# A two-layer kernel with routed experts: layer 1 rows go to a fixed region per expert, in three routing batches

## The reference

```python
router_logits = h @ Wr + br                       # [2048, 8]
gates = max(softmax(router_logits)); idx = argmax(router_logits)
xn = layernorm(h) * ln_g + ln_b
y = (relu(xn @ W1[idx] + b1[idx]) @ W2[idx] + b2[idx]) * gates
x = x + gb * y
```

## Time and profile before

| | before |
|---|---|
| median of 3 runs | 422.17 us |
| the profiled execution | 422.7 us, of which 420.7 us lie between the first and the last instruction (the span) |
| PE busy, PEld busy | 309.1 us (73%), 226.5 us (54%) |
| DVE busy | 288.0 us (68%) |
| ACT busy | 173.2 us (41%) |
| POOL busy | 189.0 us (45%) |
| mean granted TensorE clock | 0.774 |

### The profile page before, as it was taken

The page is one execution under the profiler, slowest core; times in us unless marked ns, Lnnn a source line. Parts: engine busy times, 40 slices in busy tenths (PEclk is TensorE's granted clock), DMA queues, the critical chain, the costliest instruction groups (busy, mean ns, idle before and its releaser), DMA issues.

```text
span 420.7 us, 7639 instructions
## 1 busy us (share of the span) xinstructions
PE 309.1 (73%) x2168; PEld 226.5 (54%) x2169; DVE 288.0 (68%) x819; ACT 173.2 (41%) x333; POOL 189.0 (45%) x318
## 2 busy tenths in 40 slices
PE   1784889888991789969779799988877000999960
PEld 1582316734240333258679799976565000989960
DVE  7587993889379999438885567635895860578850
ACT  1124563223750217885255355546255210545520
POOL 8573782390037670000267545455143474045450
PEclk9877555555595555888999999999996555799995
DMA  2499900000001112001121422158800123233310
GB/s 83 66 353 368 322 22 1 0 2 1 2 21 44 44 51 35 0 2 42 49 65 55 80 72 63 37 166 240 248 2 1 43 85 101 61 87 87 86 47 0
DMA packets 37805, 32.93 MB, mean 78 GB/s; under 512 B 10765, under 2 KB 28770, under 8 KB 37776
## 3 DMA queue, kind: packets, MB, share of 16 engines
q1 hardware_dynamic: 33792, 25.10, 21.6%
q0 software_dynamic: 3936, 7.49, 5.6%
q10 hardware_dynamic: 48, 0.00, 0.0%
HBM read 19.50 MB, written 13.98 MB: 80 GB/s over the span
## 4 chain that ended last, share of the span: by engine, by line
PE 45%; DVE 27%; issue 8%; DMA 5%; POOL 5%; ACT 4%; SPq 2%; DVEq 2%; POOLq 0%
PE ps L1353 9%; PE ps L1364 8%; PE ps L1181 6%; PE ps L1176 5%; DVE mx L1958 5%; PE ps L1156 4%; POOL rows L624 4%; PE ps L1203 2%; PE ps L1132 2%; ACT wide L855 2%; DVE hb L2094 2%; SPq L302 2%; DVE ps L2220 1%; PE ps L1337 1%; DMA rows<-token_rows,posu 1%
## 5 line engine op out<-in xcount | busy, mean ns | idle before, releaser
L624 POOL DMA_INDIRECT rows<-token_rows,posu x48 | 50.2, 1046 | 52.5 <-DVE posu L1855 25.5
L636 POOL DMA_INDIRECT back<-ys,places x39 | 38.6, 990 | 75.0 <-DVE ys L2105 69.8
L1364 PE MATMUL ps<-w_out,hg 128*128 x496 | 65.2, 276 | 0.0
L1364 PEld LDWEIGHTS ps<-w_out,hg 128*128 128x128 f32 x496 | 60.1, 192 | 0.2
L2094 DVE TENSOR_TENSOR hb<-ps,b_in 128x512 f32<-128x512 f32 x62 | 42.6, 687 | 25.4 <-PE ps L1353 25.2
L953 ACT ACTIVATE hg<-hb 128x512 f32<-128x512 f32 x62 | 39.1, 630 | 38.8 <-DVE hb L2094 35.0
L1958 DVE TENSOR_REDUCE mx<-ps 128x2 f32<-128x512 f32 (+2 forms) x48 | 44.4, 949 | 5.4 <-PE ps L1156 5.1
L1353 PE MATMUL ps<-xsT,w_now 128*128 128x128 f32 x256 | 38.3, 297 | 6.5 <-DVE hb L2094 4.1
L1337 PE MATMUL ps<-ident,xs 128*128 128x128 f32 x62 | 17.7, 292 | 33.9 <-DMA xs<-rows 33.9
L1156 PE MATMUL ps<-feat,qs 64*128 64x281 bf16 (+2 forms) x128 | 33.3, 431 | 12.0 <-DVE mx L1958 7.6
L839 ACT COPY qs<-ps 128x768 bf16<-128x768 bf16 (+1 forms) x21 | 15.3, 728 | 59.6 <-PE ps L1132 59.6
(11 more groups left out here) (404 smaller groups left out, 588.0 us busy)
## 6 DMA issues: line engine op xcount, KB each, us to landing
rows<-blank SPq DMA_DIRECT2D x20, 260.0 KB, 7.1
xs<-rows SPq DMA_DIRECT2D x62, 64.0 KB, 1.9
w_in<-in_L_ffn_w_fc SPq DMA_DIRECT2D x1, 2048.0 KB, 14.9
w_in<-in_L_ffn_W SPq DMA_DIRECT2D x1, 2048.0 KB, 10.6
rest<-rows SPq DMA_DIRECT2D x23, 65.0 KB, 1.9
token_rows<-in_L_attn_x SPq DMA_DIRECT2D x1, 832.0 KB, 8.3
wmod<-in_L_wmod SPq DMA_DIRECT2D x2, 384.0 KB, 4.5
rows<-token_rows,posu POOLq DMA_INDIRECT x48, 2.4
```

The lines of the kernel that those rows point to most:

```text
L624: pool.indirect_dma_start(ROWS[l], bass.IndirectOffsetOnAxis(ap=posu[:, k, j:j + 1], axis=0), token_rows[:, j, 0:WIDTH[l]], None).then_inc ...
L636: pool.indirect_dma_start(where, bass.IndirectOffsetOnAxis(ap=target[r] if l else places[:, t, :].bitcast(U32)[:, 0:1], axis=0), ys[:, r, ...
L1364: mm = pe.matmul(ps[:, 6 + c % 2, 0:D], hg[:, c % RING, n * P:(n + 1) * P], w_out[:, bass.ds(e * NB + n, 1), :], start=(n == 0), stop=(n = ...
```

## The change

1. `rows1` gets a region of 2048 rows for each of the 8 experts and one spare block: 129 blocks of 128 rows in place of 23. A row's place is 2048 times its expert plus its rank, so no total is needed before rows are sent. All 129 blocks are cleared; the clearing of `rows1` moves behind the loads of layer 0's expert weights on SP.
2. Layer 1 is routed in three batches (token tiles 0-2, 3-10, 11-15). PE sums a row's rank in PSUM (`regions`, `rank`); DVE has `choose_one`, `place_one`, `gate_one` for each batch. The scale arithmetic is shared out anew between POOL and DVE, and the rows of the last two pieces that DVE normalised are ACT's now.
3. `plan_tiles` on DVE writes, for each of the 23 tiles, the number of its block to `src_tile`. SP reads this number into a register (`value_load`) for each tile; its loop over layer 1 tiles is written out as `second_tiles`, with `xs` and `rest` of **the same tile** in one step.
4. The gate row that multiplies `w_out` in `gate_weights(1)` is read from PSUM.
5. Some semaphores are merged, and `rows_dve` replaces two.

```diff
+BATCHES = [(0, 3), (3, 11), (11, 16)]
+BATCH_OF = [0, 1, 1, 2, 2]
+SPARE = NE * NT
...
-            return -(-NTILE[l] * WIDTH[l] // (4 * ROW0))
+            return -(-(SPARE + 1 if l else T0) * WIDTH[l] // (4 * ROW0))
...
             clear_rows(sp, 0)
+            load_experts(sp, 0)
             clear_rows(sp, 1)
-            load_experts(sp, 0)
...
-                def next_rest(k, c):
-                    if l:
-                        sp.wait_ge(sem(f"ys_sent{c % RING}"), 16 * (k + (c // RING + 1 + earlier(l, c % RING))))
-                        load_rest(k + 1, c)
...
+            def second_tiles():
+                src = ROWS[1].rearrange("(t p) c -> p t c", p=P)
+                at = [None] * T1
+                def load_rest(t):
+                    sp.dma_start(rest[t % RING][:], src[:, bass.ds(at[t], 1), D:D + REST]).then_inc(
+                        sem(f"rest_loaded{t % RING}"), 16)
+                sp.wait_ge(sem("placed"), 4)
+                for t in range(RING):
+                    at[t] = sp.value_load(src_tile[0:1, t:t + 1], min_val=0, max_val=SPARE)
+                sp.wait_ge(sem("scattered_all"), 16 * NT)
+                for t in range(RING):
+                    load_tile(1, at[t], t)
+                for t in range(RING):
+                    load_rest(t)
+                for t in range(RING, T1):
+                    at[t] = sp.value_load(src_tile[0:1, t:t + 1], min_val=0, max_val=SPARE)
+                    sp.wait_ge(sem("xs_used"), T0 + t - RING + 1)
+                    load_tile(1, at[t], t)
+                    sp.wait_ge(sem(f"ys_sent{t % RING}"), 16 * (t // RING + earlier(1, t % RING)))
+                    load_rest(t)
+            first_tiles()
+            second_tiles()
...
-            def step_scales(c, summed, done):
-                lo, hi = STEPS[c]
-                scales(SLOT_OF[lo], SLOT_OF[lo] + hi - lo, summed, done, c + 1)
-            for c in range(3):
-                step_scales(c, "summed_1", "scaled_1")
-            pool.wait_ge(sem("summed_1"), 5)
-            root(8, 13).then_inc(sem("roots"), 1)
-            for c in range(2):
-                step_scales(c, "summed_2", "scaled_2")
-            pool.wait_ge(sem("slots_all"), 1)
-            pool.wait_ge(sem("gates_all"), 1)
+            scales(*STEPS[0], "summed_1", "scaled_1", 1)
+            scales(*STEPS[1], "summed_1", "scaled_1", 2)
+            scales(*STEPS[0], "summed_2", "scaled_2", 1)
+            scales(*STEPS[2], "summed_1", "scaled_1", 3)
+            scales(*BATCHES[2], "summed_1", "scaled_1", 4)
+            scales(*STEPS[1], "summed_2", "scaled_2", 2)
             pool.wait_ge(sem("cleared1"), 16 * clears(1))
             for c, (lo, hi) in enumerate(STEPS):
...
+                pool.wait_ge(sem("placed"), BATCH_OF[c] + 1)
+                pool.wait_ge(sem("gates_all"), BATCH_OF[c] + 1)
...
             step_rows(0)
             keep_x(0)
             step_rows(1)
             keep_x(1)
             modulated(1)
+            step_sent(0)
             step_rows(2)
+            keep_x(2)
+            gate_exp(0)
             modulated(2)
-            keep_x(2)
+            step_rows(3)
+            step_rows(4)
             modulated(3)
             modulated(4)
-            act.wait_ge(sem("rows1_dve"), 3)
             keep_x(3)
             keep_x(4)
-            step_sent(0)
-            act.wait_ge(sem("lg_shifted"), 1)
-            act.activation(lg2[:], lg2[:], ACT.Exp).then_inc(sem("lg_exp"), 1)
-            for c in range(1, len(STEPS)):
-                step_sent(c)
+            gate_exp(1)
+            step_sent(1)
+            step_sent(2)
+            gate_exp(2)
+            step_sent(3)
+            step_sent(4)
+            act.copy(ps[:, 6, 0:D], modrow[1][:, GB, :]).then_inc(sem("row_placed"), 1)
...
+            def regions(b):
+                lo, hi = BATCHES[b]
+                pe.matmul(ranks(b), onesb[:], region[:].unsqueeze(1).to_broadcast([P, hi - lo, NE]), start=True, stop=False)
+                for j in range(lo):
+                    pe.matmul(ranks(b), onesb[:], picked(j, hi - lo), start=False, stop=False)
+            def rank(b):
+                lo, hi = BATCHES[b]
+                pe.wait_ge(sem("chosen"), 3 + b)
+                for j in range(lo, hi - 1):
+                    pe.matmul(ranks(b)[:, j + 1 - lo:hi - lo, :], onesb[:], picked(j, hi - 1 - j), start=False, stop=False)
+                pe.matmul(ranks(b), before[:], chosen[:, lo:hi, :], start=False, stop=True).then_inc(sem("ranked"), 1)
...
             modes_out(4)
+            pe.wait_ge(sem("x_kept"), 6)
+            logits(0, 0)
             turn_back(1)
-            pe.wait_ge(sem("x_kept"), 6)
-            logits(0)
-            logits(1)
+            pe.wait_ge(sem("chosen"), 3)
+            regions(0)
+            rank(0)
             turn_f(2)
-            logits(2)
+            pe.wait_ge(sem("placed"), 1)
+            logits(1, 1)
+            logits(1, 2)
+            turn_back(2)
+            pe.wait_ge(sem("x_kept"), 7)
+            regions(1)
             turn_f(3)
             turn_f(4)
-            logits(3)
-            logits(4).then_inc(sem("logits1"), 1)
-            for c in (2, 3, 4):
-                turn_back(c)
-            count("all")
+            rank(1)
+            logits(2, 3)
+            logits(2, 4)
+            pe.wait_ge(sem("rows_all"), 1)
+            regions(2)
+            turn_back(3)
+            turn_back(4)
+            pe.wait_ge(sem("rows_all"), 2)
+            totals(0, BATCHES[2][0])
+            rank(2)
+            totals(BATCHES[2][0], NT).then_inc(sem("ranked"), 1)
...
-                gb = modrow[l][:, GB, :].unsqueeze(1)
+                gb = ps[:, 6, 0:D].unsqueeze(1) if l else modrow[l][:, GB, :].unsqueeze(1)
+                if l:
+                    v.wait_ge(sem("row_placed"), 2)
...
+            def choose_one(b):
+                lo, hi = BATCHES[b]
+                n = hi - lo
+                bc = lambda t: t.unsqueeze(2).to_broadcast([P, n, NE])
+                c, l, m = cand[:, lo:hi, :], lg2[:, lo:hi, :], top[:, 0, lo:hi]
+                pl = ps[:, 0, 0:n * NE].rearrange("p (j e) -> p j e", e=NE)
+                v.wait_ge(sem("logits1"), b + 1)
+                then(v.tensor_reduce(m, pl, AX.X, ALU.max))
+                signal(v.tensor_tensor(l, pl, bc(m), ALU.subtract), "lg_shifted", b + 1)
+                then(v.scalar_tensor_tensor(out=c, in0=l, scalar=0.0, in1=e_rank[:].unsqueeze(1).to_broadcast([P, n, NE]), op0=ALU.is_equal, op1=ALU.mult))
+                then(v.tensor_reduce(posf[:, lo:hi], c, AX.X, ALU.max))
+                signal(v.tensor_tensor(chosen[:, lo:hi, :], c, bc(posf[:, lo:hi]), ALU.is_equal), "chosen", 3 + b)
+            def place_one(b):
+                lo, hi = BATCHES[b]
+                v.wait_ge(sem("ranked"), b + 1)
+                then(v.tensor_tensor(cand[:, lo:hi, :], ranks(b), chosen[:, lo:hi, :], ALU.mult))
+                then(v.tensor_reduce(posf[:, lo:hi], cand[:, lo:hi, :], AX.X, ALU.add))
+                signal(v.tensor_copy(posu[:, 0, lo:hi], posf[:, lo:hi]), "placed", b + 1)
+            def gate_one(b):
+                lo, hi = BATCHES[b]
+                v.wait_ge(sem("lg_exp"), b + 1)
+                then(v.tensor_reduce(posf[:, lo:hi], lg[:, lo:hi, :], AX.X, ALU.add))
+                signal(v.reciprocal(token_rows[:, lo:hi, GATE], posf[:, lo:hi]), "gates_all", b + 1)
+            def plan_tiles():
+                bank, at = TOTALS_AT
+                v.wait_ge(sem("ranked"), 4)
+                c = cmp_f[:].rearrange("p (e j) -> p e j", e=NE)
+                then(v.tensor_tensor(c, ps[:, bank, at:at + NE].unsqueeze(2).to_broadcast([P, NE, NT]),
+                                     step128[:].unsqueeze(1).to_broadcast([P, NE, NT]), ALU.is_gt))
+                then(v.tensor_reduce(ntile[:], c, AX.X, ALU.add))
+                running(bound[:, 0:NE], ntile[:], 0.0)
+                then(v.tensor_scalar(slack[:], ntile[:], -1.0, float(NT), ALU.mult, ALU.add))
+                then(tile_experts(0, T1, NE))
+                c = cmp_e[:, 0:T1 * NE].rearrange("p (t n) -> p t n", n=NE)
+                then(v.tensor_tensor(c, c, slack[:].unsqueeze(1).to_broadcast([P, T1, NE]), ALU.mult))
+                then(v.tensor_reduce(srcf[:, 0:T1], c, AX.X, ALU.add))
+                then(v.tensor_tensor(srcf[:, 0:T1], srcf[:, 0:T1], tidx[:, 0:T1], ALU.add))
+                signal(v.tensor_scalar(src_tile[:, 0:T1], srcf[:, 0:T1], float(SPARE), None, ALU.min), "placed", 4)
...
+            sent_sums(0, ("summed_2", 1))
+            step_sums(2, 3)
             step_sums(3)
-            step_sums(4)
-            for c in range(2):
-                sent_sums(c, ("summed_2", c + 1))
-            v.wait_ge(sem("roots"), 2)
-            for c in (3, 4):
-                for j in range(*STEPS[c]):
-                    at = SLOT_OF[j]
```

(77 more changed lines are left out.)

223 lines of the change are left out of this document (102 added, 121 removed).

## The result

The changed kernel takes 550.51 us (median of 4 runs, 545.89 to 552.98), the kernel before 422.89 us beside it (4 runs): a ratio of 1.312, interval 1.302 to 1.322. The profiled execution took 549.4 us, with a span of 547.7.

A forecast was written before the change was run, and what follows sets the result against it. Bound by a chain through POOL's scatter queue, then the expert loop at 2.01 us a tile. Span 420.7 - 8.9 + 133.0 + 2.5 = 547.3, plus 1.5 to the runs' median: 549 us, range 526 to 568.

The forecast's parts named there:

- SP's order makes the loop a ring: Layer 1 expert loop: SP's wait for a tile's send stands ahead of the next tile's xs; +133.0 us.
- Rival 3: SP in layer 1's loop isn't held by send waits, only the routing saving is left; 413 us, chance 0.05.
- Length of the way: Layer 1 loop, transpose to next transpose through down, DVE, POOL's send, rest and xs: 9.45 us at low clock.
- The register load: SP, between rest and xs: reading the block number adds 0.35 us, DVE's price; that step becomes 1.0 us.
- Rival 2: SP's read of the block number costs PE's maximum, 1.26 us; 565 us, chance 0.07.
- The clock: PE in layer 1's loop: granted 0.50 through idling; down takes 1.92 instead of 1.06 us, the transpose 0.11 more.
- Rival 1: PE keeps a granted clock of 1.00 in layer 1's loop, 8.48 us a step; 530 us, chance 0.18.
- The routing's gain: Before layer 1's loop: POOL's last scatter starts at 343.3 instead of 352.16; 8.9 us saved, bounds 11.2 and 7.5.
- the wait for piece 2's second turn: Layer 1 routing, DVE waiting for PE: end at 321.4, bounds 319.1 and 322.75; fourth scatter starts at 327.9.
- The stretched scatters: POOL, layer 1: two scatters of 2.01 and 1.90 us instead of 0.96 end with PSUM operand; saving 5.5 if they stay.
- The clearing: Clearing 129 blocks of rows1: ends near 91 us under idle DMA, costs nothing; 38 us without that cover.
- The tail: End of layer 1's loop: five down and two up remain, the first three or so at low clock; +2.5 us.

The follow-up runs named there:

- the run with added work: Changed kernel with 36 identity transposes added on PE ahead of the first product of 16 layer 1 tiles; 538.9 us, ratio 1.277.
- lead of 4: Changed kernel with only SP's loop put back: behind xs of tile t the wait and rest of tile t - 4; 415.53 us, ratio 0.985.
- the gate row: Version with a lead of 4, the row multiplying w_out in layer 1 read from SBUF as in the kernel before; 417.76 us, ratio 0.992.
- the turn put first: Version with a lead of 4, PE's turn_back(2) moved ahead of logits(1, 2); 413.35 us, ratio 0.980.

## Why the prediction was right, step by step

Predicted 549 us, measured 550.5; the sum was made against the span, 547.3, and the span is 547.7. The mechanism is the one predicted. That the two spans agree to 0.4 us is partly luck, as the items below show: terms that were too large and too small cancelled.

- **SP's order makes the loop a ring: right, and shown.** The same edit alone gives 552 us on the kernel before, undoing it gives 416 on the changed one. Rival 3 (SP isn't held, 413 us) is out, though its number for the rest of the change was near.
- **Length of the way: 9.45 us predicted, 161.16/17 = 9.48 measured.** Its parts, as means of the 17 turns: transpose to `rest` 6.39 predicted, 6.53 measured (`down` takes 2.01 to 2.07 us in all turns but the first, where 1.92 was taken); `rest` to `xs` 1.0 and 1.11; `xs` to PE 2.06 and 1.84. Two parts were 0.25 us short and one 0.22 long, so the agreement to 0.03 is luck. The first turn, mostly at the high clock, 8.48 against 8.32. The 18 steps: 169.1 against 169.48.
- **The register load: taken from the right engine, with a small error.** The price was DVE's 0.35 us for four registers; SP's for one is 0.27, with 0.15 of register work behind it. Taking it from the loop saves 0.46 us a turn. Rival 2 (1.26 us, as on PE) is out. So is the floor of 600 ns of the Trainium skill (DMA: Bandwidth & Descriptors, Latency and other measured facts) for the load by itself; a whole reading with its register work and check does come to 0.60 us where 23 stand in a row (13.7 us).
- **The clock: right.** Nine of the 17 turns lie wholly at 0.50; in the other eight it is 0.68 in the mean, but `down` takes 2.01 to 2.07 us there too, and the turn 9.42 in place of 9.53. Rival 1 (all at 1.00) is out. Beside the turns at 1.00 of the run with added work a turn at 0.50 costs 0.96 us more, where 0.97 was taken. The 2 us of PE work in a round hold for the high clock only: in the first turn PE is busy for 2.06 us, in the next, at 0.50, for 4.25.
- **The routing's gain: 8.9 us predicted, 6.1 measured; this is the term that was mis-sized.** The first transpose is 8.16 us earlier, but layer 1's sums began 2.03 earlier already (DVE at 309.26, in place of 311.29). The version with a lead of 4 shows the same 6 us in its median. And over the profiles the last scatter starts at 346.9 in the mean of eight with the changed routing (343.95 to 349.93; the gate row and the turn put first are left out), at 353.2 in the mean of the two with the old one: 6.3 us. The step that failed is the wait for piece 2's second turn. I put its end at 321.4 and bounded it by 322.75; corrected for the 2.03 it came at 324.2. The rows of PE and DVE:

```profile
315.90 1.12 PE L1506 MATMUL ps<-ident,y 128*128 128x128 f32 x4 [0.95 <-ACT y L930]
316.95 0.69 PE L1525 MATMUL ps<-br_row,ones 1*128 1x64 f32 x2
317.56 3.58 PE L1529 MATMUL ps<-wrl,feat 128*128 128x8 f32 x16
321.00 1.09 PE L1517 MATMUL ps<-ident,feat 128*128 128x128 f32 x4
```
```profile
322.20 0.89 DVE L2213 BATCH_NORM_STATS2 stats<-ps 128x6 f32<-128x128 f32 x4 [5.19 <-PE ps L1517]
```

  Sixteen logits products, at 0.22 us each, stand ahead of the turn. The second batch moved eight of them, those of piece 1, behind `turn_f(2)`; piece 2's eight stand ahead of the turn in the kernel before too. There, with the granted clock at 1.00, such a product took half the time:

```profile
314.11 1.63 PE L1508 MATMUL ps<-wrl,feat 128*128 128x8 f32 x14
```

  My upper bound was the time at which all logits are done in the kernel before, where PE makes the turns behind them: a bound from another order. Putting the turn ahead of eight of them took 1.7 of the 5.19 us off the wait (3.47 left), which shows this part of the 2.8. What makes up the rest wasn't tried: the low clock is one candidate (0.50 from 314.6 to 324, where the kernel before had 1.00 until 318.7; at 0.12 us a product the sixteen would take some 1.9 us in place of 3.6, an estimate), the wait for ACT's rows (0.95) another.
- **The stretched scatters are gone because of PSUM: right**, argued then, shown now. Without it the gain would have been 4 us. (Of the 15 steps between the scatters 13 are not stretched, not fourteen; the spacing of 1.28 was worked out with 15.)
- **The clearing: right.** It ends at 92 us, 91 was predicted, and doubling it costs nothing that the runs can tell.
- **The tail: 2.5 predicted, 2.02 measured.** The clock was back at 0.69 in its first 8 us.
- **The 2.03 us at the start were not in the sum.** In this execution PE had a clock of 1.00 between 64 and 68 us, where it was 0.50 before: eight products of 128x68 took 1.22 us at 66.47, and 1.97 at 65.72 before. In the nine other profiles of the changed kernel and its variants it was 0.50 there as well. These ten profiles put layer 1's first scatter anywhere between 319.2 and 325.2 us, two executions of one kernel (the lead of 4) at 322.19 and 320.10. So the 2.03 us lie within the spread of executions and are not shown to come from the change. They made the sum look better than it was: the gain was too large by 2.8, the start 2.0 earlier than assumed.

## What to carry to other kernels

On an in-order queue, ask of each wait not only what it waits for but which loads stand behind it: a buffer's reuse wait that moves ahead of the next tile's first load turns a pipeline into a ring, whose turn is the way round divided by the tiles that may be on it (9.48, 4.66 and 3.25 us for one, two and three here), until another limit takes over. Its length can be added up from the rows of the kernel before, step by step; here each step came out within 0.22 us, and the sum closer than its parts. For a bound on a wait, take the order that the changed kernel has on the engine that is waited for, and not a time at which the same products are done in the old order.

## What the hardware showed that I had not expected

- The place of one operand (one row of 128 numbers, broadcast) of a DVE multiplication decides whether indirect DMA instructions beside it on POOL take 0.96 us or 2.12 and 1.90, while the multiplication itself takes 4.5 us either way.
- PE busy for 6.72 us of 8 had a granted clock of 0.79, and for 5.68 of 8, fifty microseconds later in the same loop, 1.00. The busy share of a stretch alone did not tell its clock. Part of it is an effect of the clock: the first stretch holds 45 products, the second 50.
- Adding 36 products to each of 16 turns made the kernel 11.6 us faster, since the products on the path ran at a higher clock: eight of `down` took 1.06 to 1.15 us where the clock was 1.00, and 1.92 to 2.07 in the changed kernel at 0.50.
